# Moving the Gram stage's first loads into the stage before it, and the waits for the last stores to their readers

## What is computed

```python
kv = einsum('oc,bchw->bohw', qkv_w, x)          # 1x1 projection, keys and values
kv = dw3x3(kv, qkv_conv_w)                      # 3x3 depthwise
k, v = split(kv, 2, axis=1)
q = idwt2(dw3x3(dwt2(x)))                       # wavelet, three depthwise 3x3, inverse
q, k, v -> (b, 8 heads, 16, h * w)
q = q / norm(q);  k = k / norm(k)
attn = softmax(einsum('bhdn,bhen->bhde', q, k) * temperature)
out = proj_w @ (attn @ v)
```

## Time and profile before

| | before |
|---|---|
| median of 3 runs | 1396.62 us (1393.0 to 1396.84) |
| the profiled execution | 1390.65 us |
| its span, first to last instruction | 1389.0 us |
| PE / DVE / ACT / POOL busy | 84% / 74% / 64% / 32% |
| first stage, by the trace | 0 to 189 us |
| Gram stage | 189 to 888 us |
| attention and convolutions | 888 to 1389 us |

### The profile page before, as it was taken

The page is one execution under the profiler, slowest core; times in us unless marked ns, Lnnn a source line. Parts: engine busy times, 40 slices in busy tenths (PEclk is TensorE's granted clock), DMA queues, the critical chain, the costliest instruction groups (busy, mean ns, idle before and its releaser), DMA issues. The chain is left out here.

```text
span 1389.0 us, 33923 instructions
## 1 busy us (share of the span) xinstructions
PE 1170.3 (84%) x12756; PEld 922.8 (66%) x12756; DVE 1024.9 (74%) x1771; ACT 888.5 (64%) x1574; POOL 440.8 (32%) x473
## 2 busy tenths in 40 slices
PE   0999929999999999999999999536999997999900
PEld 0555518999999999999999998313555554555500
DVE  6677418999999999999999998156766743063394
ACT  0677837888888889888888985011344254766382
POOL 6100024565565655556566563120000010000010
PEclk9999969999999999999999999768999999999955
DMA  9976793444444545544454441458777330000079
GB/s 331 416 305 272 305 193 91 122 114 128 134 106 129 149 105 128 136 121 119 128 143 98 132 129 40 141 189 285 273 255 237 91 120 0 1 1 0 0 297 400
DMA packets 148679, 221.00 MB, mean 159 GB/s; under 512 B 115624, under 2 KB 116788, under 8 KB 144192
## 3 DMA queue, kind: packets, MB, share of 16 engines
q1 hardware_dynamic: 137456, 152.26, 36.3%
q0 software_dynamic: 6480, 47.19, 8.9%
q10 hardware_dynamic: 4608, 19.67, 4.1%
HBM read 131.84 MB, written 87.20 MB: 158 GB/s over the span
## 5 line engine op out<-in xcount | busy, mean ns | idle before, releaser
L1675 PE MATMUL b_conv_bank<-b_sign,wsign 128*128 (+1 forms) x1728 | 295.8, 328 | 10.5 <-ACT b_sign L1455 7.7
L1675 PEld LDWEIGHTS b_conv_bank<-b_sign,wsign 128*128 128x128 bf16 x1728 | 168.1, 97 | 140.6 <-issue 28.3
L756 POOL TENSOR_TENSOR b_vacc<-b_vacc 128x576 f32<-128x576 f32 x128 | 180.5, 1410 | 192.5 <-ACT b_vacc L850 191.7
L989 PE MATMUL b_bank<-b_tkh,b_kt 96*96 96x100 f16 x1536 | 219.5, 209 | 2.3 <-DVE b_tml L970 2.3
L991 PE MATMUL b_bank<-b_tkh,b_kt 96*96 96x100 f16 x1536 | 219.3, 209 | 0.0
L990 PE MATMUL b_bank<-b_tkl,b_kt 96*96 96x100 f16 x1536 | 219.2, 209 | 0.0
L989 PE MATMUL b_bank<-b_yh,b_tmh 96*96 96x200 f16 x768 | 193.3, 252 | 16.0 <-DVE b_yl L954 10.7
L947 DVE SCALAR_TENSOR_TENSOR b_value_sum<-b_vin,b_vtaps,b_value_sum 128x576 f32<-128x576 f32 x256 | 206.6, 807 | 0.0
L1474 ACT CAST b_y<-b_conv_bank 128x384 f32 (+1 forms) x192 | 91.2, 478 | 170.4 <-PE b_conv_bank L1675 168.3
L989 PEld LDWEIGHTS b_bank<-b_tkh,b_kt 96*96 96x96 f16 x1536 | 192.1, 125 | 3.7 <-DVE b_tml L970 2.5
L991 PEld LDWEIGHTS b_bank<-b_tkh,b_kt 96*96 96x96 f16 x1536 | 192.3, 125 | 0.0
(11 more groups left out here) (214 smaller groups left out, 2556.0 us busy)
## 6 DMA issues: line engine op xcount, KB each, us to landing
b_vin<-value_projection_scratch SPq DMA_DIRECT2D x32, 686.0 KB, 5.8
keys_scratch<-b_khl SPq DMA_DIRECT2D x24, 784.0 KB, 3.5
value_projection_scratch<-b_vout ACTq DMA_DIRECT2D x24, 784.0 KB, 4.6
b_kt<-keys_scratch SPq DMA_DIRECT2D x128, 147.0 KB, 3.0
b_xraw<-in_x SPq DMA_DIRECT2D x128, 144.0 KB, 5.3
values_scratch<-b_vacc SPq DMA_DIRECT2D x32, 576.0 KB, 3.4
b_values<-values_scratch SPq DMA_DIRECT2D x48, 384.0 KB, 3.8
out<-xs SPq DMA_DIRECT2D x25, 576.0 KB, 6.8
```

Source lines behind the costliest of these rows:

```text
L756: nc.gpsimd.tensor_tensor(whole, whole, room, ALU.add).then_inc(s_padd, 1)
L989: nc.tensor.matmul(out, w_hi, m_hi, start=first, stop=False)
L1675: ins = nc.tensor.matmul(cbank[k % NBK][:, 0:CH].rearrange("p (r c) -> p r c", c=W), p["wsign"][nth // NIMG][:, t * C:(t + 1) * C], padded ...
```

## The change

- `b1_x` now holds three images. Image 0 lies in a tile `x_first` of its own, which lives through the Gram stage. In it, once image 0 is projected, lie the Gram stage's `xraw`, `kt`, the five placing constants, `eprod`, the high half of `ya`, `gcor`, `rm` and `rk`, one behind the other (`EARLY`, 9215 of 9216 floats). `vtaps` and `null_cols` have small tiles of their own.
- In SyncE's list of the first stage, behind the key store n = 6 (image 1's first): the store of `key_unscale`, the seven constants, and the x rows of the groups 0 and 1. Behind the key store n = 18 (image 3's first): a wait for the key stores of images 0 to 2, and their six loads of key rows.
- The first stage ends without a wait for its key and value stores. The Gram stage's SyncE loads slab 0 (image 0's values only), waits for all key stores, loads image 3's key rows of the groups 0 and 1 and slab 1, and waits for all value stores. ScalarE waits for all stores ahead of its first group.
- GpSimd zeroes `ya` behind its first spreading of taps; VectorE no longer waits for it, ScalarE does ahead of its first group. ScalarE's two casts of x stand between the lead copies.

```diff
+STORES = 3
+STORED = NIMG * 6 // STORES * 16
+def early_tiles(p):
+    tiles, at = {}, 0
+    for name, (rows, n, dt) in EARLY.items():
+        wide = n if dt == F32 else -(-n // 2)
+        part = p["x_first"][0:rows, at:at + wide]
+        tiles[name] = part if dt == F32 else part.bitcast(F16)[:, 0:n]
+        at += wide
...
-        x = sb("b1_x", [C, NIMG, HW])
+        x = sb("b1_x", [C, NIMG - 1, HW])
...
             for n in range(NIMG * NPC):
...
-            sp.wait_ge(s_ready, 1)
-            sp.dma_start(d["key_unscale"], key_unscale[:]).then_inc(s_us, 16)
-            for s_one in s_st[0]:
-                sp.wait_ge(s_one, NIMG * NPC // NBUF * 16)
+                if n == NPC:
+                    sp.wait_ge(s_ready, 1)
+                    sp.dma_start(d["key_unscale"], key_unscale[:]).then_inc(s_us, 16)
+                    sp.wait_ge(s_hi, 2 * NCH)
+                    early = early_tiles(p)
+                    for name in ("ana", "map_place", "key_place", "map_diag", "key_diag"):
+                        sp.dma_start(early[name], d[name]).then_inc(p["s_c"], 16)
+                    sp.dma_start(early["vtaps"], d["value_taps"]).then_inc(p["s_c"], 16)
+                    sp.dma_start(early["null_cols"], d["null_cols"].partition_broadcast(W)).then_inc(p["s_c"], 16)
+                    for i in range(2):
+                        for im in range(NIMG):
+                            load_x_rows(sp, d, early, im, i, i, p["s_xin"][i])
+                if n == (NIMG - 1) * NPC:
+                    for s_one in s_st[0]:
+                        sp.wait_ge(s_one, (NIMG - 1) * NPC // NBUF * 16)
+                    for i in range(2):
+                        for im in range(NIMG - 1):
+                            load_key_rows(sp, d, early, im, i, i, p["s_kin"][i])
             sp.wait_ge(s_us, 16)
...
-            for s_one in s_st[1]:
-                act.wait_ge(s_one, NIMG * NPC // NBUF * 16)
             act.wait_ge(s_zs, NIMG * 2 * 16)
...
+            for s_one in p["s_st"][1]:
+                sp.wait_ge(s_one, STORED // NIMG)
+            load_slab(0, 0)
+            for s_one in p["s_st"][0]:
+                sp.wait_ge(s_one, STORED)
             for i in range(2):
-                load_rows(xraw, d["x_rows"], s_xin, i, i)
-                load_keys(i, i)
-                load_slab(i * SLAB * WP, i)
+                load_key_rows(sp, d, early, NIMG - 1, i, i, s_kin[i])
+            load_slab(SLAB * WP, 1)
+            for s_one in p["s_st"][1]:
+                sp.wait_ge(s_one, STORED)
...
-            for t in ya:
-                nc.gpsimd.memset(t[:], 0.0).then_inc(s_z, 1)
-            pool.wait_ge(s_z, 2)
...
             spread_taps(0, 0)
+            for t in ya:
+                nc.gpsimd.memset(t[:], 0.0).then_inc(s_z, 1)
...
-            act.wait_ge(s_z, 2)
             act.wait_ge(s_c, 7 * 16)
...
-            for part in range(2):
-                high_x(0, 0, part)
             for m, (kind, j) in enumerate(lead):
+                if m in (1, 2):
+                    high_x(0, 0, m - 1)
                 act.wait_ge(s_pe, m + 1)
...
+            act.wait_ge(s_z, 2)
+            for s_one in p["s_st"][0] + p["s_st"][1]:
+                act.wait_ge(s_one, STORED)
             body(0, 0, 0, FIRST)
```

## The result

| | before | changed |
|---|---|---|
| median | 1395.46 us (7 runs) | 1385.72 us (7 runs, 1381.24 to 1388.22) |
| ratio of the runs | | 0.9931, 95% interval 0.9913 to 0.9949 |
| the profiled execution, its span | 1390.65, 1389.0 us | 1383.91, 1382.0 us |
| first instruction of the Gram stage | 189.29 | 186.77 |
| VectorE's first tap of the Gram stage | 210.35 | 199.96 |

The changed kernel is 9.7 us faster, 0.7%, where 17.5 was forecast. The gain at the seam is there; by the profiled execution close to half of it was paid back in the first stage.

A forecast was written before the change was run, and what follows sets the result against it. It took TensorE's unfed 28.3 us between the first stage's last value store and the first Gram loop matmul as what counts; 10.7 + 7.85 - 0.5 - 0.5 = 17.5 us off 1396.6 gave 1379.1, range 1374 to 1388.

The forecast's parts named there:

- Part 1: First stage's exit: ScalarE and SyncE no longer wait for stores, Gram stage entered at 178.6 instead of 189.29; gain 10.7 us.
- Part 2: Gram stage's entry: constants and x rows already in, ScalarE's wait of 7.95 us falls to about 0.1; gain 7.85 us.
- Parts 3 and 4: Gram stage's start: lead work unchanged, taken as 0; waits for keys, slabs and stores hidden, cover thin for slab 0 alone.
- Part 5: Image 1: key_unscale's store, seven constants and eight x loads between key stores; cost 0 to 8 us, taken +0.5.
- the first rival: Image 1: the 512-byte store holds traffic and loads, ScalarE waits 0 to 8 us, middle 4; 1383 us, chance 0.14.
- Part 6: Image 3: six key loads between two key stores about 5 us apart; cost 0, at most 1 us.
- Part 7: Gram stage's entry: engines leaving busy code straight into the next stage's; unseen cost 0 to 2.6 us, taken +0.5.
- The clock: TensorE's clock at the stage seam: its fall may come later or not at all; worth 0 to 1 us, taken as 0.
- Slower by addresses: Gram loop: operands at multiples of four bytes slow 2,240 matmuls; 1406 us at 12 ns each, chance 0.03.
- The likeliest case: Whole kernel: full gain of 16 to 19.5 us, own range 1376 to 1382 us, chance 0.60.

The follow-up runs named there:

- waits_only: Changed kernel without its early loads: Gram-stage loads in the old order, waits at the readers, store of key_unscale ahead of the first key store; 1388.47 us, ratio 0.9949.

## Why the prediction was right or wrong

**Part 1, the exit: right.** 0.47 us from the end of the last issue to the first instruction, 0.55 assumed. That the slow landings were `key_unscale`'s, read there from its being the odd one out, was shown by moving it: the way from the last value store's issue into the next stage fell from 11.5 us to 4.1.

**Part 2, the loads: right.** 7.85 us forecast; normalisation starts 0.08 us behind the entry, and the trace of `waits_only` puts the whole at 8.65.

**Parts 3 and 4: right.** 7.65 us of lead work (7.67), 5.46 from ScalarE's tap to VectorE's (5.44). The slab, whose cover the prediction called thin, made nobody wait; nor did the last keys, although they took 6.2 us, not 3.9.

**Part 5 is the step that failed.** It was taken as +0.5 and measured 8.2, the upper end of its bounds. The reason given, that "the cover holds in each single case", was true: the hold alone and the loads alone each cost nothing there. The mistake was to test the covers one by one although the change puts both between the same two key stores. The hold stops the loads too, the queue fills, and the next key store is late twice: it isn't issued for 10 us, and it then takes 9.5 us to land, 6 more than usual, while what had been held is moved (275 to 439 GB/s in each us from 98 to 108). By an estimate from these rows either delay alone costs little: issued at 98.11 and landed in 3.5 us the store costs 1.8 us, issued at 88 and landed in 9.5 us nothing. That is the first rival. It had the store leave at 92 to 98.4 and land 3.5 to 9.5 us later, and the measured 98.11 and 9.5 are the upper ends of both; it put the wait at 0 to 8 us with 4 in the middle, and its chance at 0.14. Its sum was sound, and it should have been the likeliest. The objection that VectorE's pace absorbs some of it did not hold: ScalarE came to the buffer at 99.8, as before. Of the worst cases that part 5 named, one did not come: the key store just ahead of the small store landed in 3.6 us, not 9.5.

The sentence from the Trainium skill (DMA: Bandwidth & Descriptors, Back-pressure in remote DMA) that stalled writes stall the engine's other queues fits: in the windows above, stores and loads together move 45 GB/s while the small store is out. These are transfers of the core itself, which that section does not speak of, and that it is the same mechanism is not shown.

**Part 6: right,** no wait in image 3. **Part 7: 0 and not 0.5;** nothing of the entry was late.

**The clock: right in size, incomplete in place.** It was at half from about 188 until 201, worth nothing as assumed: from VectorE's first tap to the group's store of values it is 20.3 us before and after. Not foreseen was that the later seam between two groups is an edge: the clock fell there in nine of the ten variants, at 1.2 to 2.85 us each, and stayed up in the one with the fill. In the changed kernel it did not.

**Slower by addresses:** refuted. The matmuls that read the high half of y take 247 ns at least and 250 in the middle, against 247 and 249 in the earlier trace rows, and the 704 that read the tap blocks 233 and 235, as before:

```profile
L1025 PE MATMUL b_bank<-x_first,b_tmh x768: 247/250/369, 204.2 to 853.8; 96*96 96x200 f16 x192
```

Sum by the profile: 18.55 less 8.2 is 10.35; measured are 10.4 at VectorE's first tap and 10.35 at the end of the Gram stage. The median lies 6.6 us above the forecast of 1379.1, and the 7.7 us by which part 5 was off cover it. That the time fell within 1374 to 1388 is owed to the width of that range, which took in part of the first rival. The likeliest case's own range, 1376 to 1382, missed it.

## What to carry to other kernels

When a change puts several things between two steps of one queue, add their worst cases up and hold the sum against the cover; covers that hold singly say nothing. Transfers that are early and free in bytes still take places in the queue of the engine that issues them, so put them where that engine has time, a few at a time: the same loads, spread, gave 18.1 us, where in one place they gave 9.7 and 12.5. And look at the odd small transfer whenever large ones beside it land late.

## What the runs showed of the hardware

A store of 128 four-byte pieces into 512 bytes of DRAM took 8.9 to 9.8 us to land beside stores and 11.1 to 12.8 beside the first loads. For 4 to 7 us, while it was out and up to 2 us longer, the stores and loads of all queues in use together moved at most 61 GB/s. 128 pieces of eight bytes 512 bytes apart took 3.1 us and held nothing, nor did 128 of 64 bytes side by side. Two such stores at once took 0.5 us more than one.

Behind an idle stretch of 2.6 us TensorE's granted clock fell from 1.00 to 0.50 (2.4 to 1.2 GHz) in nine of twelve executions and stayed there 3.4 or 6.8 us, at the cost of 1.2 to 2.85 us of the group. With matmuls in that stretch it stayed up in the one execution profiled.
